# A graph and mixture-of-experts kernel: the choice of experts made inside the scoring block, relation tiles shared out anew

## What is computed

```
x = x + gnn0(layernorm(x))      # 3 rounds of: mean over neighbours @ Wl + x @ Wr, scaled, relu (not in the last)
x = x + ffn0(layernorm(x))      # 16 experts, hidden 512, relu
x = x + gnn1(layernorm(x))      # Clifford messages h[src] * relation[edge_type], gated, summed
x = x + ffn1(layernorm(x))      # 8 experts, hidden 1024, gelu

# the choice of two experts per node
ffn0: logits = x @ gate_w + gate_b; top2 of logits; weights = softmax(top2)
ffn1: probs = softmax(x @ Wr + br); top2 of probs; weights = top2 / sum(top2)
```

## Time and profile before

| | us |
|---|---|
| median of 3 runs | 3071.25 (3070.46 to 3072.17) |
| profiled execution, as timed | 3068.61 |
| its span | 3067.0 |
| busy: TensorE / weight loads | 2439.1 / 1911.3 |
| busy: VectorE / ScalarE / GpSimd | 1782.3 / 1450.7 / 1744.9 |

### The profile page before, as it was taken

How to read it: one execution, slowest core, us unless ns; L and a number is a source line. 1 busy time by engine, 2 the same in 40 slices (tenths; PEclk the granted TensorE clock), 3 DMA queues, 4 the chain that set the end, 5 groups by cost and what they waited for, 6 DMA issues and landing times. The chain is left out here.

```text
span 3067.0 us, 52892 instructions
## 1 busy us (share of the span) xinstructions
PE 2439.1 (80%) x14195; PEld 1911.3 (62%) x14195; DVE 1782.3 (58%) x5132; ACT 1450.7 (47%) x3766; POOL 1744.9 (57%) x1702
## 2 busy tenths in 40 slices
PE   0769999989998499841877877777777775899997
PEld 0446666767686388740655555555555555799996
DVE  7679888667787511046776666666666666211110
ACT  0356676555565233323544444444444424455553
POOL 1447777367776345423777777777777750233332
PEclk9989999999998599975999898999899987899998
DMA  6647777478887433434666666666666632443232
GB/s 227 208 139 227 222 222 214 135 221 258 252 259 236 162 116 108 153 114 153 194 189 182 184 187 186 185 185 187 177 189 186 185 106 102 123 106 78 48 65 65
DMA packets 289373, 516.56 MB, mean 168 GB/s; under 512 B 79344, under 2 KB 137057, under 8 KB 287084
## 3 DMA queue, kind: packets, MB, share of 16 engines
q0 software_dynamic: 86192, 225.20, 28.4%
q1 hardware_dynamic: 185532, 267.85, 26.6%
q10 hardware_dynamic: 17392, 20.46, 2.1%
HBM read 381.08 MB, written 137.11 MB: 169 GB/s over the span
## 5 line engine op out<-in xcount | busy, mean ns | idle before, releaser
L726 POOL DMA_INDIRECT agg_r_rows<-h_table,parts_and_x x832 | 829.7, 997 | 336.8 <-issue 224.0
L817 PE MATMUL agg_r_sums<-agg_r_rows,agg_r_onehot 128*128 128x257 f32 x1664 | 492.3, 425 | 262.6 <-DVE agg_r_rows L798 166.3
L817 PEld LDWEIGHTS agg_r_sums<-agg_r_rows,agg_r_onehot 128*128 128x128 f32 x1664 | 310.5, 205 | 399.8 <-issue 326.7
L686 ACT ACTIVATE agg_r_gap<-iota,parts_and_x 128x128 f32<-128x128 f32 x832 | 286.6, 392 | 449.2 <-PE agg_r_sums L817 420.3
L780 DVE TENSOR_TENSOR acc<-acc,agg_r_sums 128x257 f32 (+1 forms) x834 | 351.8, 422 | 136.6 <-PE agg_r_sums L817 50.9
L1733 POOL DMA_INDIRECT rl_buf<-r_table,kinds x272 | 301.6, 1109 | 125.0 <-issue 71.1
L2129 PEld LDWEIGHTS f_pH<-f_xT,f_w 128*128 128x128 f32 x2816 | 332.7, 195 | 39.6 <-ACT f_xT L2207 17.8
L2129 PE MATMUL f_pH<-f_xT,f_w 128*128 128x128 f32 x2816 | 346.6, 280 | 9.9 <-ACT f_xT L2207 4.5
L831 PE MATMUL agg_r_spread<-xn 128*128 128x257 bf16 x2664 | 341.1, 287 | 0.0
L1733 POOL DMA_INDIRECT rm_buf<-r_table,kinds x270 | 264.4, 979 | 121.3 <-issue 74.1
L2148 PE MATMUL f_pY<-f_w,f_hT 128*128 128x256 f32 x1408 | 326.0, 381 | 7.9 <-DMA f_w<-in_L_ffn_w 7.8
(11 more groups left out here) (419 smaller groups left out, 3608.6 us busy)
## 6 DMA issues: line engine op xcount, KB each, us to landing
agg_r_rel<-relation_rows SPq DMA_DIRECT2D x305, 260.0 KB, 3.1
relation_rows<-rl_buf SPq DMA_DIRECT2D x136, 260.0 KB, 3.2
relation_rows<-rm_buf SPq DMA_DIRECT2D x135, 260.0 KB, 3.3
agg_r_rows<-h_table,parts_and_x POOLq DMA_INDIRECT x832, 3.3
f_w<-in_L_ffn_W SPq DMA_DIRECT2D x18, 512.0 KB, 5.5
f_w<-in_L_ffn_W SPq DMA_DIRECT2D x9, 1024.0 KB, 4.8
f_w<-in_L_ffn_w SPq DMA_DIRECT2D x30, 256.0 KB, 3.3
f_w<-in_L_ffn_w SPq DMA_DIRECT2D x15, 512.0 KB
```

The lines of the kernel that those rows point to most:

```text
L686: last = nc.scalar.activation(gap[:, n % HOT, t, :], c.iota[:, 0:P], ACT.Abs, bias=c.tab["b_near"][:, column(g) + t:column(g) + t + 1])
L726: pool.indirect_dma_start(rows[:, n % SLOTS, t, :], None, table, bass.IndirectOffsetOnAxis(ap=indices[:, t:t + 1], axis=0)).then_inc(s_row ...
L817: last = nc.tensor.matmul(sums[:, (2 * n + t) % BANKS, 0:used], onehot[:, n % HOT, t, :], rows[:, n % SLOTS, t, 0:used], start=True, stop= ...
```

## The change

The choice moves from `feed_forward` into `norm_and_gate`, and is made in two parts, for tiles 0 to 19 when their scores are in, and for tiles 20 to 24 when theirs are. The scores of the last five tiles go to another PSUM bank. In the second expert layer the softmax moves along; its two exponentials stand in ScalarE's queue behind the copies of tiles 23 and 24. The small block of `matrix_and_layer` is taken out; its two tables are made by VectorE in `gnn0_start` from numbers that lie there already. The shares become 48, 272, 270 and 20; in `gnn0_start` SyncE has three stores ahead of each z store and the 24th behind the last.

```diff
-SHARES = (36, 272, 270, 32)
+SHARES = (48, 272, 270, 20)
...
+class Choice:
+
+    FIRST = NT - J
...
+    def highest(self, v, st, logits, ts):
+        high = self.small[:, 0, ts]
+        st.link(v.tensor_reduce(high, logits[:, ts, :], AX.X, ALU.max))
+        return v.tensor_tensor(logits[:, ts, :], logits[:, ts, :], bc(high.unsqueeze(2), [P, ts.stop - ts.start, self.ne]), ALU.subtract)
+
+    def shares(self, v, st, logits, ts):
+        total, part = self.small[:, 1, ts], self.small[:, 2, ts]
+        st.link(v.tensor_reduce(total, logits[:, ts, :], AX.X, ALU.add))
+        st.link(v.reciprocal(part, total))
+        st.link(v.tensor_tensor(logits[:, ts, :], logits[:, ts, :], bc(part.unsqueeze(2), [P, ts.stop - ts.start, self.ne]), ALU.mult))
+
+    def choose(self, c, v, st, logits, ts):
+        wide = [P, ts.stop - ts.start, self.ne]
+        for t in range(ts.start, ts.stop):
+            last = v.max(self.top[:, t, :], logits[:, t, :])
+        st.link(last)
+        for t in range(ts.start, ts.stop):
+            last = v.max_index(self.idx[:, t, :], self.top[:, t, :], logits[:, t, :])
+        st.link(last)
+        for q in range(2):
+            last = v.tensor_copy(self.idx_f[:, q, ts], self.idx[:, ts, q])
+        st.link(last)
+        for q in range(2):
+            last = v.tensor_tensor(self.pick[:, q, ts, :], bc(c.iota[:, 0:self.ne].unsqueeze(1), wide),
+                                   bc(self.idx_f[:, q, ts].unsqueeze(2), wide), ALU.is_equal)
+        st.link(last)
+        st.link(v.tensor_tensor(self.both[:, ts, :], self.pick[:, 0, ts, :], self.pick[:, 1, ts, :], ALU.add))
+        if ts.stop == NT:
+            v.tensor_scalar(self.both[:, NT - 1, :], self.both[:, NT - 1, :], c.alive[:, 0:1], None, ALU.mult)
...
+        late_scores = product[:, 1, :] if update else k.ps(f"{name}_late_scores", [P, 512])
...
                 def score(t):
                     pe.wait_ge(s_xT, t + 1)
+                    to, at = score_at(t)
+                    if update and t == choice.FIRST:
+                        pe.wait_ge(s_used, NT)
...
                         nc.scalar.activation(xT[:, t % 2, :, :].rearrange("p k c -> p (k c)"), x_turns[:, t % 2, 0:D], ACT.Copy).then_inc(s_xT, 1)
+                    if choice.softmax and t in (NT - 2, NT - 1):
+                        q = t - NT + 2
+                        ts = (slice(0, choice.FIRST), slice(choice.FIRST, NT))[q]
+                        act.wait_ge(s_high, q + 1)
+                        nc.scalar.activation(logits[:, ts, :], logits[:, ts, :], ACT.Exp).then_inc(s_exp, 1)
...
-                dve.wait_ge(s_score, NT)
-                v.tensor_tensor(logits[:, :, :], scores[:, 0:NT * ne].rearrange("p (t n) -> p t n", n=ne),
-                                bc(gate_bias[:, :].unsqueeze(1), [P, NT, ne]), ALU.add)
+                for q, ts in enumerate((slice(0, choice.FIRST), slice(choice.FIRST, NT))):
+                    count = ts.stop - ts.start
+                    dve.wait_ge(s_score, ts.stop)
+                    src = (scores, late_scores)[q][:, 0:count * ne].rearrange("p (t n) -> p t n", n=ne)
+                    st.link(v.tensor_tensor(logits[:, ts, :], src, bc(gate_bias[:, :].unsqueeze(1), [P, count, ne]), ALU.add))
+                    if choice.softmax:
+                        choice.highest(v, st, logits, ts).then_inc(s_high, 1)
+                        dve.wait_ge(s_exp, q + 1)
+                        choice.shares(v, st, logits, ts)
+                    choice.choose(c, v, st, logits, ts)
...
                 eb.starts(v, st)
+                v.tensor_scalar_add(c.numbers[:, :], c.wide_iota[:, 0:CODES], 1.0)
+                v.tensor_copy(c.strip_ids[:, :], c.wide_iota[:, 0:STRIPS])
...
-                    work.store(sp, 8 + 2 * b, 10 + 2 * b)
+                    work.store(sp, 8 + 3 * b, 11 + 3 * b)
                     sp.wait_ge(s_z0, (b + 1) * J)
...
-                work.store(sp, 8 + 2 * NJ, work.pairs)
+                work.store(sp, 8 + 3 * NJ, work.pairs)
...
-            whole = kk.sb("b_whole", [P, CODES], I32)
-            s_n = kk.sem("b_whole_set")
-            with nc.Block() as block:
-
-                @block.gpsimd
-                def _(pool):
-                    Core.clear(pool)
-                    pool.iota(whole[:, :], pattern=[[1, CODES]], base=0, channel_multiplier=0).then_inc(s_n, 1)
-
-                @block.vector
-                def _(dve):
-                    dve.wait_ge(s_n, 1)
-
-                    nc.vector.tensor_scalar_add(numbers[:, :], whole[:, :], 1.0)
-                    nc.vector.tensor_copy(strip_ids[:, :], whole[:, 0:STRIPS])
```

More of the change, by code:

```diff
@@ L839, in _, with __init__ @@
                     beside.tensor(pe, n)
-def norm_and_gate(nc, c, name, ne, gate, gate_bias, logits, xn_table, update=None, tables=(), relation=None):
+class Choice:
+    FIRST = NT - J
+    def __init__(self, room, ne, softmax):
+        self.ne, self.softmax = ne, softmax
+        sizes = [NT * 8, NT * 8, 2 * NT, 3 * NT, 2 * NT * ne, NT * ne]
+        top, idx, idx_f, small, pick, both = (room[:, sum(sizes[:q]):sum(sizes[:q + 1])] for q in range(6))
+        self.top = top.rearrange("p (t n) -> p t n", t=NT)
+        self.idx = idx.bitcast(U32).rearrange("p (t n) -> p t n", t=NT)
+        self.idx_f = idx_f.rearrange("p (q t) -> p q t", q=2)
+        self.small = small.rearrange("p (q t) -> p q t", q=3)
+        self.pick = pick.rearrange("p (q t e) -> p q t e", q=2, t=NT)
+        self.both = both.rearrange("p (t e) -> p t e", t=NT)
+    def highest(self, v, st, logits, ts):
[25 more added lines that the diff above has]
+            v.tensor_scalar(self.both[:, NT - 1, :], self.both[:, NT - 1, :], c.alive[:, 0:1], None, ALU.mult)
@@ L844, in norm_and_gate @@
+def norm_and_gate(nc, c, name, ne, gate, gate_bias, logits, xn_table, choice, update=None, tables=(), relation=None):
     PRODUCTS, LATE = 3, 2 * J
@@ L1962, in _, with experts @@
                         nc.scalar.activation(shift[:, :], vecs[:, 4, :], ACT.Sqrt).then_inc(s_root, 1)
-def experts(nc, c, I, name, ne, nf, tiles, softmax_first, w1, b1, w2, b2, logits, xn_table, norm, act_fn, h_table=None, out=None):
+def experts(nc, c, I, name, ne, nf, tiles, choice, w1, b1, w2, b2, xn_table, norm, act_fn, h_table=None, out=None):
     ys = c.dram(f"{name}_ys", [NP + P if out is not None else 2 * NP + tiles * P, D])
@@ L1984, in feed_forward @@
     with Core(nc) as k:
[L1985 to L1989 removed]
+        top, pick, both, softmax_first = choice.top, choice.pick, choice.both, choice.softmax
         place = k.sb(f"{name}_place", [P, NT, ne])
@@ L2037, in feed_forward @@
             loads += [(lg[:, :, :], norm[0]), (lb[:, :, :], norm[1])]
-        s_link, s_a, s_b, s_m, s_rank, s_hits, s_tiles, s_named, s_found, s_token, s_etab, s_bias = (
-            k.sem(f"{name}_r{x}") for x in ("link", "to_act", "to_dve", "both", "rank", "hits", "tiles", "named", "found", "token",
+        s_link, s_a, s_b, s_rank, s_hits, s_tiles, s_named, s_found, s_token, s_etab, s_bias = (
+            k.sem(f"{name}_r{x}") for x in ("link", "to_act", "to_dve", "rank", "hits", "tiles", "named", "found", "token",
                                             "etab", "bias"))
```

72 lines of the change are left out of this document (23 added, 49 removed).

## The result

| | before | changed | ratio, 95% interval |
|---|---|---|---|
| median, first comparison (5 runs each) | 3070.46 | 3055.66 (3048.99 to 3057.85) | 0.9946 [0.9932, 0.9961] |
| median, later comparison (23 and 5 runs) | 3071.85 | 3053.60 (3053.10 to 3058.13) | 0.9948 [0.9935, 0.9961] |
| span of the profiled execution | 3067.0 | 3054.0 | |
| busy: TensorE / VectorE / GpSimd | 2439.1 / 1782.3 / 1744.9 | 2431.9 / 1788.4 / 1752.6 | |

The changed kernel is 16 us faster, as forecast (3055.3; 3050 to 3061). By the intervals the gain is 12 to 21 us, so the total alone can't check the small terms of the sum. The distances between instructions in the trace can: in the two traces of the changed kernel they repeat within 0.02 us, in the three of the kernel before within 0.3.

The account below looks back on a forecast made before the run. Stage boundaries, chains of one engine at a time, were taken as the bound, not throughput. The terms -12.75 -0.25 -4.0 +1.0 = -16.0 from the median 3071.25 gave 3055.3 us, range 3050 to 3061.

Parts of the forecast that it names:

- Part 1: End of ng0, first scoring block: 12 relation tiles leave, stores land by 1021.2, so SyncE no longer ends the block.
- rival (e): The change does not do what it says, for instance ng0 still closed by a late transfer: about 3064; chance 0.02.
- Part 2: Choice among 16 experts made in ng0, mostly while TensorE still scores: first rank matmul 12.75 us earlier.
- Rival (a): The choice in ng0 does not overlap scoring, the block ends 6.3 us later, total 3061.6; chance 0.06.
- rival (c): Small terms go well: last store free, boundary under 0.3 us, TensorE's clock granted higher after ng0: 3052; chance 0.10.
- Part 3: Choice among 8 experts with softmax in ng1, waiting for the exponential behind tile 23's copy: 0.25 us saved.
- Part 4: Between gnn0_start and the matrix stage's first load: removing the small block saves 4.0 us.
- Part 5: 12 relation tiles enter gnn0_start; the 24th store behind the last z store costs 1.0 us (ends 0 to 7.6).
- Rival (d): Gather ring in gnn0_start runs in series, ending 42 us after the old end: 3097, slower than before; chance 0.02.
- Rival (b): Small terms go wrong together: last store +2.0, ng1's exponential later by 1.4, overlap short by 1: 3059; chance 0.12.

Follow-up runs that it names:

- e1: Changed kernel with the old shares of relation tiles (36, 272, 270, 32) and old store order in gnn0_start; 10.8 us [7, 14] under the kernel before.
- e6: Changed kernel with ScalarE's first exponential in ng1 behind the copy of tile 21 instead of 23; 18.4 us [14, 23] under the kernel before.
- e3: Kernel before with only the small block taken out, its two tables made in gnn0_start; 2.1 us [-1, 5] under the kernel before.
- e4: Changed kernel with the 24th relation store of gnn0_start ahead of the last z store; 19.1 us [14, 24] under the kernel before.
- e9: Changed kernel with 24th store ahead of last z store, first exponential behind tile 21's copy, 18 added TensorE products per expert block; 3050.93 us, ratio 0.9926.

## Why the prediction was right

**Part 1** held: in the changed kernel SyncE's last relation stores of ng0 are issued from 1010.81, before the last score, SyncE is through 3.7 us before the block ends, and e1 shows what they cost when they are not moved (B 8.59 instead of 3.88). With B at 3.88 rival (e) is out.

**Part 2**, -12.75 forecast, measured -12.6. The lengths 6.9 and 2.8 us, made of fixed parts and an elementwise rate, came out as 6.92 and 2.88, and the boundary as 0.30. Rival (a) is out: VectorE's first instruction follows the score of tile 19 while TensorE goes on. The clock term of rival (c) is out too: the first rank group took 1.67 us (1.70 before), at a granted clock of 0.50 in both. One sign was wrong: the profile names the block's boundary as releaser of the rank matmul, and not VectorE, whose work now ends inside ng0.

**Part 3**, -0.25 forecast, measured -0.15. Its mechanism, the table load behind the copy of tile 23, is what e6 shows. The forecast idle time of VectorE, some 4.5 us, came out as 4.63.

**Part 4**, -4.0 forecast, measured -3.75 (e3). It was taken 0.25 too large: the z store landed at 155.27, not 155.1, and with no block between, the first load came 0.41 us behind the landing (e3), not 0.3. **Part 5**, +1.0 forecast, measured +1.15 (the changed kernel against e1 and e3), of which e4 gets back 0.87. The 1.0 was the middle between two estimates, so its closeness is luck in part: the store was issued 0.42 us behind the z store and not 0.8, and landed after 3.9. Rival (d), the ring in series, is out: the last z store follows its predecessor by 9.46 to 9.47 us in all thirteen traces, e4 with its store put ahead among them.

**Rival (b)** had its three terms go wrong together. None did: the store cost 1.15 and not 2, ng1's exponential came no later than forecast, and the overlap in ng0 came as forecast.

**The sum** was 16.0; the places give 15.4, the ratios 16.6 and 16.0 with intervals of about 4 us to either side. So the closeness of the total is partly luck. Three things of the prediction were too narrow. It took the spread of a run for 1 us, from three runs that lay 1.7 us apart; the kernel before has since run from 3065.4 to 3080.4. It gave absolute times as signs: the first load at 156 to 157, and a z store later than 152 as a sign of error. The z store itself moves from trace to trace (150.5 to 152.3 in the old order, 150.3 to 152.7 in the new), so the first load came at 155.69 in the first trace of the changed kernel and at 157.66 in its second, whose z store at 152.74 would have counted as error. And it called an expert loop or an aggregation that changes its length by over 2 us a sign of error: the aggregation (+3.5) and the first expert loop (-3.4) did so in the first pair of traces, and the kernel before does it against itself (aggregation 1091.1, 1095.4, 1093.4).

**What stays open.** Whether the changed order lengthens the aggregation by some 3 us in the mean. For it: the means, 1092.6 in five traces and 1096.2 in eight; if the thirteen were split five to eight by chance, a difference as large would come up in 4 splits of 100. Against: the shortest of all, 1090.6, is the changed kernel's, and the totals, which would then be about 12 us apart, are 16 apart. Taken whole, the rest of the program did not change its length: the span less A, B and C is 3032.8 us in the mean of the five traces and 3033.5 in the mean of the eight, with the single traces 10 to 11 us apart in each. A longer aggregation would thus be made up elsewhere; the first expert loop, from its first product to the aggregation, is 2.3 us shorter in the mean of the six unfilled changed traces (348.5 against 350.8). Why is not known. Nor do the totals show whether e4 and e6 are worth the 3.8 us of their places.

## What to carry to other kernels

Two things can hold a block open, and to remove one gives only the distance to the other: price both alone and together, as 7.5, 7.9 and 12.6 here. When work is moved ahead into another engine's queue, count what stands before it there; two places in ScalarE's queue were worth 2.9 us, and the whole move without them 0.15. Before a filler goes ahead of a signal, see who waits for the signal: here the weight loads started 2.8 us later. Where single executions scatter by several us, judge a small edit by distances between neighbouring instructions, and by more than one trace: B and C of the same order repeat to 0.2 us or better, the start of a loop does not.

## What the runs showed of the hardware

**A gather on GpSimd does not always cost the same, and the aggregation's length follows it.** Its 832 gathers in four kernels: before, the changed kernel, the same again, and e9 (busy us, mean ns, idle before):

```profile
L726 POOL DMA_INDIRECT agg_r_rows<-h_table,parts_and_x x832 | 829.7, 997 | 336.8 <-issue 224.0 <-PE agg_r_sums L809 83.6 <-PE agg_r_sums L817 29.3
```

```profile
L726 POOL DMA_INDIRECT agg_r_rows<-h_table,parts_and_x x832 | 833.1, 1001 | 336.7 <-issue 224.6 <-PE agg_r_sums L809 83.4 <-PE agg_r_sums L817 28.7
```

```profile
L726 POOL DMA_INDIRECT agg_r_rows<-h_table,parts_and_x x832 | 829.2, 997 | 336.6 <-issue 224.9 <-PE agg_r_sums L809 83.3 <-PE agg_r_sums L817 28.4
```

```profile
L726 POOL DMA_INDIRECT agg_r_rows<-h_table,parts_and_x x832 | 839.2, 1009 | 336.6 <-issue 227.7 <-PE agg_r_sums L809 83.3 <-PE agg_r_sums L817 25.6
```

The idle time is the same in all (336.6 to 336.8), the busy time is not, and the stage took 1091.1, 1094.6, 1090.6 and 1100.6 us: it follows GpSimd's busy time one to one. In all thirteen traces it is that busy time plus 261.3 to 261.5 us. The median gather is 0.953 us in all four; the slow ones among them, up to 1.67 us, make the difference. GpSimd is then what bounds the aggregation, and the granted TensorE clock, 0.91 to 0.92 in these stretches, leaves no mark on its length.

The slow gathers have a companion. Of the 10816 in the thirteen traces 2002 took over 1.0 us, and 1942 of these overlap VectorE's product of gathered rows and relation rows (line 798 of the kernel before, both operands in SBUF). Of the 1048 beside an idle VectorE none was slow, and none of the 1462 beside only its sum into `acc`, which reads one operand from PSUM. No run took the product away, so the cause is not shown.

**The start of an expert loop has two lengths.** The first 10 us from the first hidden product of the first loop, in e4 and then in a repeat of the kernel before (columns as in the stretches above):

```profile
1059.79:1069.79 10.00, 8.74 (x41) 8.24 (x42) 0.00 (x0) 2.44 (x10) 0.95 (x1) 0.58 0.60 209
```

```profile
1070.34:1080.34 10.00, 8.75 (x48) 7.79 (x49) 0.38 (x2) 3.06 (x12) 0.95 (x1) 0.76 0.64 218
```

The granted clock is 0.58 in one and 0.76 in the other, with TensorE busy equally long, and the first result comes after 11.0 and 9.6 us. What decides between the two in an unfilled kernel was not found; both occur in either order of the work.
